# A graph network kernel: count rows gathered as 16-bit integers and turned by transposing transfers, and the mean's transposes moved amid the products of the node's own rows

## The reference, cut to what matters

```python
h = jnp.maximum(_layernorm(x, axis=-1), 0.0)
x = x + _L0_gnn_ref(h, edge_index, ...)           # attention over neighbours
h = jnp.maximum(_layernorm(x, axis=-1), 0.0)
x = x + _L1_gnn_ref(h, ...)

def _L1_gnn_ref(x, gate_W, gate_b, Wl, bl, Wr, edge_index):
    gates = softmax(x @ gate_W + gate_b); top_v, top_i = top_k(gates, 2)
    def sage_conv(h, W_l, b_l, W_r):
        aggr = segment_sum(h[src], dst) * inv_deg   # mean over neighbours
        return aggr @ W_l + b_l + h @ W_r
    for e in range(4):
        h = x
        for l in range(2):
            h = relu(sage_conv(h, Wl[e, l], bl[e, l], Wr[e, l]))
        ...
    out = sum of the two picked experts' h, each times its gate
```

## Time and profile before

| | us |
|---|---|
| median of 3 runs | 862.31 (857.92 to 866.23) |
| the profiled execution | 863.82 |
| its span, first to last instruction | 862.1 |
| TensorE busy | 752.3 (87%) |
| VectorE busy | 444.7 (52%) |
| ScalarE busy | 254.6 (30%) |
| POOL busy | 176.2 (20%) |

### The profile page before, as it was taken

One profiled execution on the slowest core, in us unless ns is written; L12 is line 12 of the kernel. 1 busy time (PEld: TensorE's weight loads), 2 busy tenths in 40 slices (PEclk: granted clock), 3 DMA queues, 4 the chain that ended last, 5 costly groups with the idle time before them and its releaser, 6 DMA issues.

```text
span 862.1 us, 11919 instructions
## 1 busy us (share of the span) xinstructions
PE 752.3 (87%) x3620; PEld 611.0 (71%) x3621; DVE 444.7 (52%) x1088; ACT 254.6 (30%) x516; POOL 176.2 (20%) x160
## 2 busy tenths in 40 slices
PE   1019877499997999998999999989999999999994
PEld 0007655388886888876777777768888888888883
DVE  6999999678876415572263343433223332323230
ACT  0113444555555425141141221312211221212120
POOL 6602433300000001055000000023322332233201
PEclk9999899889997999999999999999999999999997
DMA  4200000011124014769989695369934993449910
GB/s 127 84 0 2 0 0 0 1 59 59 62 84 149 2 49 127 241 195 275 304 285 331 223 348 172 105 197 272 327 94 109 274 330 93 110 108 246 343 22 5
DMA packets 46809, 125.30 MB, mean 145 GB/s; under 512 B 7280, under 2 KB 7412, under 8 KB 46752
## 3 DMA queue, kind: packets, MB, share of 16 engines
q1 hardware_dynamic: 29072, 81.58, 29.0%
q0 software_dynamic: 9232, 26.17, 12.1%
q10 hardware_dynamic: 8448, 16.78, 5.6%
HBM read 72.19 MB, written 53.20 MB: 145 GB/s over the span
## 4 chain that ended last, share of the span: by engine, by line
PE 71%; DVE 18%; DMA 4%; issue 3%; DVEq 1%; ACT 1%; POOL 0%; POOLq 0%; SPq 0%; ACTq 0%
PE ps L1417 15%; PE ps L1419 15%; PE ps L1418 15%; PE ps L1714 6%; PE ps L1713 5%; DVE onehot_g L1025 5%; PE ps L1579 3%; DVE column L1013 3%; PE ps L1580 3%; PE ps L1641 3%; DMA raw<-in_L_gnn_Wr 2%; DVE onehot_p L966 2%; PE ps L1685 1%; PE ps L1724 1%; PE ps L1510 1%
## 5 line engine op out<-in xcount | busy, mean ns | idle before, releaser
L1714 PE MATMUL ps<-slots,CTs 125*128 x230 | 90.9, 395 | 0.0
L1713 PE MATMUL ps<-slots,CTs 125*128 x207 | 81.6, 394 | 0.0
L1345 DVE CAST CTs<-ps 125x512 fp32r<-125x512 f32 (+1 forms) x69 | 37.3, 595 | 85.1 <-PE ps L1641 62.0
L611 POOL DMA_INDIRECT out<-tg,rec x23 | 36.9, 1605 | 192.3 <-ACT tg L877 175.5
L1252 DVE TENSOR_TENSOR he_t<-ps,b_b 125x512 f32<-125x512 f32 x40 | 27.5, 690 | 86.1 <-PE ps L1419 73.8
L1390 DVE TENSOR_TENSOR tm<-ps,b_b 128x512 f32<-128x512 f32 x23 | 15.9, 691 | 102.3 <-PE ps L1419 102.3
L1417 PE MATMUL ps<-W,h2T_hi 128*125 128x512 f32 x160 | 64.2, 401 | 2.8 <-DVE W L1220 2.8
L827 ACT ACTIVATE slots<-he_t 125x512 fp32r<-125x512 f32 x40 | 25.3, 635 | 132.3 <-DVE he_t L1252 113.3
L1418 PE MATMUL ps<-W,h2T_hi 128*125 128x512 f32 x160 | 63.8, 399 | 0.0
L1419 PE MATMUL ps<-W,h2T_lo 128*125 128x512 f32 x160 | 63.7, 398 | 0.0
L1417 PE MATMUL ps<-W,agT_hi 128*125 128x512 f32 x160 | 63.6, 397 | 0.0
(11 more groups left out here) (268 smaller groups left out, 1722.9 us busy)
## 6 DMA issues: line engine op xcount, KB each, us to landing
he_d<-slots SPq DMA_DIRECT2D x30, 448.0 KB
slots<-he_d SPq DMA_DIRECT2D x30, 448.0 KB
w_d<-slots SPq DMA_DIRECT2D x3, 4096.0 KB
slots<-w_d SPq DMA_DIRECT2D x24, 512.0 KB
t_d<-he_t SPq DMA_DIRECT2D x40, 224.0 KB
c_d<-c_nat SPq DMA_DIRECT2D x10, 546.9 KB
raw<-in_L_gnn_Wl ACTq DMA_DIRECT2D x4, 1024.0 KB
raw<-in_L_gnn_Wr ACTq DMA_DIRECT2D x4, 1024.0 KB
```

Source lines behind the costliest of these rows:

```text
L611: g.indirect_dma_start(out, bass.IndirectOffsetOnAxis(ap=i32(rec[:, i, 2:3]), axis=0), tg[i % 3][:], None, bounds_check=N - 1, oob_is_err= ...
L1345: v.tensor_copy(CTs[:, 4 * r:4 * r + n, :], ps[0:P, r, 0:n * S].rearrange("p (c n) -> p c n", n=S)).then_inc(cts_ready.sem, 1)
L1713: mm(o, CTs[:, t, :], part(k, P, t * 1024, P), start=False, stop=False)
L1714: last = mm(o, CTs[:, t, :], part(k, P, t * 1024 + D, P), start=False, stop=t == T - 1)
```

## The change

- `c_nat`, `c_d` and the gathered `crow` hold 16-bit integers. A row is 1280 numbers (ten blocks of 128, the last three of each are padding) in place of 1250: 2560 bytes in place of 5000. VectorE clears the padding once.
- `turn_rows(i)` leaves TensorE. ScalarE issues a transposing DMA, `crow` to a new buffer `CTi` (two of them), and VectorE's `counts_in` copies from `CTi` in SBUF in place of PSUM. `turn_rows(0)` is issued in the last expert of the first convolution, `turn_rows(1)` before the tile loop, `turn_rows(i+2)` at the end of ScalarE's part of tile i.
- The first gathers of counts wait for the second weight of the last expert being cut (`w_lo_ready`), no longer for `wl_done`. `b2_b` moves to where `crow` was, so SP's load of it waits for `wl_done`.
- `turn_means(i)` moves behind the first 6 of the 12 own-row products in `transformed(i)`.

```diff
-        crow = [at(f"crow_{k}", [S, N], F32, o) for k, o in enumerate((147456, 152480, row_at))]
+        crow = [at(f"crow_{k}", [S, T * S], I16, o) for k, o in enumerate((R4, R4 + 2560, row_at + 1536))]
+        CTi = [at(f"CTi_{k}", [S, T, S], I16, o) for k, o in enumerate((R4 + 5120, row_at - 1024))]
-        b2_b = at("b2_b", [S, NE, D], F32, R4)
+        b2_b = at("b2_b", [S, NE, D], F32, 147456)
-        c_d = nc.dram_tensor("c_d", [N, N], F32).ap()
+        c_d = nc.dram_tensor("c_d", [N, T * S], I16).ap()
 # SP
+            sp.wait_ge(*c_pad_ready(1))
             with sp.Fori(0, QN) as q:
...
                 else:
+                    sp.wait_ge(*wl_done(NE * NGR))
                     for p, e in enumerate(PO):
                         sp.dma_start(b2_b[:, p, :], ...)
 # POOL
-            pool.wait_ge(*wl_done(NE * NGR))
+            pool.wait_ge(*w_lo_ready(KC * (cut_number(NE - 1, 1) + 1)))
             for i in range(2):
                 gather_counts(i)
...
-                    pool.wait_ge(*crow_turned(3 * (i + 1)))
+                    pool.wait_ge(*cti_in[i % 2](16 * (i // 2 + 1)))
                     gather_counts(i + 3)
 # ScalarE
+            def turn_rows(i):
+                act.wait_ge(*crow_in[i % 3](16 * (i // 3 + 1)))
+                if i >= 2:
+                    act.wait_ge(*cts_ready(3 * (i - 1)))
+                act.dma_start_transpose(CTi[i % 2][:], crow[i % 3][:]).then_inc(cti_in[i % 2].sem, 16)
...
                     load_raw(x + 1, 1)
+                else:
+                    turn_rows(0)
                 hidden(x, 2)
             act.wait_ge(*l1_done(NE * T))
+            turn_rows(1)
...
                 mean_high(i)
+                if i + 2 < NT:
+                    turn_rows(i + 2)
 # VectorE
+            v.memset(c_nat[:].rearrange("p i (t n) -> p i t n", n=S)[:, :, :, P:], 0).then_inc(c_pad_ready.sem, 1)
...
+                dve.wait_ge(*cti_in[i % 2](16 * (i // 2 + 1)))
                 for r, n in enumerate(TURNS):
-                    dve.wait_ge(*crow_turned(3 * i + r + 1))
-                    v.tensor_copy(CTs[:, 4 * r:4 * r + n, :], ps[0:P, r, 0:n * S].rearrange("p (c n) -> p c n", n=S)
-                                  ).then_inc(cts_ready.sem, 1)
+                    v.tensor_copy(CTs[:, 4 * r:4 * r + n, :], CTi[i % 2][0:P, 4 * r:4 * r + n, :]).then_inc(cts_ready.sem, 1)
 # TensorE
-                        if x == NE - 1 and t == T - 1:
-                            pe.wait_ge(*pre_ready(x * T, GROUPS[NGR - 2][-1] + 1))
-                            turn_rows(0)
...
                     for c in range(KC):
+                        if j == 0 and c == KC // 2:
+                            turn_means(i)
...
                 neighbours(i, k, he_here)
-                if i + 1 < NT:
-                    turn_rows(i + 1)
                 if i == 0:
                     turn_hidden(i)
-                turn_means(i)
                 transformed(i, k, w2_here)
```

More of the change, by code:

```diff
@@ L19 @@
 I32 = mybir.dt.int32
+I16 = mybir.dt.int16
 ALU = mybir.AluOpType
@@ L208, in gnn_kernel @@
         ag1 = at("ag1", [P, 4, D], F32, R4 + 8192)
-        c_nat = at("c_nat", [P, 2, N], F32, R3 + 20480)
+        c_nat = at("c_nat", [P, 2, T * S], I16, R3 + 20480)
         slots = at("slots", [128, 2, 18432], F32R, 0)
@@ L256, in gnn_kernel @@
         assert o6[0] <= 40960
-        crow = [at(f"crow_{k}", [S, N], F32, o) for k, o in enumerate((147456, 152480, row_at))]
+        crow = [at(f"crow_{k}", [S, T * S], I16, o) for k, o in enumerate((R4, R4 + 2560, row_at + 1536))]
+        CTi = [at(f"CTi_{k}", [S, T, S], I16, o) for k, o in enumerate((R4 + 5120, row_at - 1024))]
+        assert R4 + 3 * 2560 <= R4 + 8192 and row_at + 1536 + 2560 <= fields_at
         CTs = at("CTs", [P, T, S], F32R, 157504)
@@ L304, in gnn_kernel @@
         crow_in = signals("crow_in0 crow_in1 crow_in2")
+        cti_in = signals("cti_in0 cti_in1")
         hrow_in = signals("hrow_in0 hrow_in1 hrow_in2 hrow_in3")
-        (crow_turned, cts_ready, ctl_ready, hrow_used, heT_hi_ready, heT_lo_ready, agg_done, agn_ready, agg_turned,
+        (c_pad_ready, cts_ready, ctl_ready, hrow_used, heT_hi_ready, heT_lo_ready, agg_done, agn_ready, agg_turned,
          aggT_hi_ready, aggT_lo_ready, tm_ready, tg_ready, settled) = signals(
-            "crow_turned cts_ready ctl_ready hrow_used heT_hi_ready heT_lo_ready agg_done agn_ready agg_turned "
+            "c_pad_ready cts_ready ctl_ready hrow_used heT_hi_ready heT_lo_ready agg_done agn_ready agg_turned "
             "aggT_hi_ready aggT_lo_ready tm_ready tg_ready settled")
@@ L729, in counts_out @@
                     act.wait_ge(*c_out(0, q * 64))
-                a.activation(c_nat[:, r // 3, r % 3 * 4 * P:(r % 3 * 4 + n) * P], ps[0:P, 6 + r % 2, 0:n * P],
-                             ACT.Copy, accum_out=deg_part[:, q * 6 + r:q * 6 + r + 1]).then_inc(c_nat_ready.sem, 1)
+                first = r % 3 * 4
+                c_rows = c_nat[:, r // 3, first * S:(first + n) * S].rearrange("p (t n) -> p t n", n=S)
+                a.activation(c_rows[:, :, 0:P], ps[0:P, 6 + r % 2, 0:n * P].rearrange("p (t n) -> p t n", n=P), ACT.Copy, accum_out=deg_part[:, q * 6 + r:q * 6 + r + 1]).then_inc(c_nat_ready.sem, 1)
             for g in range(NP * QN + 3):
@@ L827, in hidden @@
                     a.activation(HE[:, t, 0:D], he_t[:, (x * T + t) % 4, :], ACT.Relu).then_inc(he_hi_ready.sem, 1)
+            def turn_rows(i):
+                act.wait_ge(*crow_in[i % 3](16 * (i // 3 + 1)))
+                if i >= 2:
+                    act.wait_ge(*cts_ready(3 * (i - 1)))
+                    with act.If(beyond):
+                        act.wait_ge(*ctl_ready(3 * (i - 1)))
+                act.dma_start_transpose(CTi[i % 2][:], crow[i % 3][:]).then_inc(cti_in[i % 2].sem, 16)
+            beyond = counts_beyond(act)
             for i in range(4):
@@ L1342, in counts_in @@
                     dve.wait_ge(*agg_done(i))
+                else:
+                    dve.wait_ge(*wl_done(NE * NGR))
+                dve.wait_ge(*cti_in[i % 2](16 * (i // 2 + 1)))
                 for r, n in enumerate(TURNS):
-                    dve.wait_ge(*crow_turned(3 * i + r + 1))
-                    v.tensor_copy(CTs[:, 4 * r:4 * r + n, :], ps[0:P, r, 0:n * S].rearrange("p (c n) -> p c n", n=S)
-                                  ).then_inc(cts_ready.sem, 1)
+                    v.tensor_copy(CTs[:, 4 * r:4 * r + n, :], CTi[i % 2][0:P, 4 * r:4 * r + n, :]).then_inc(cts_ready.sem, 1)
                 with dve.If(beyond):
@@ L1351, in counts_in @@
                     for r, n in enumerate(TURNS):
-                        v.tensor_tensor(CTl[:, 4 * r:4 * r + n, :], ps[0:P, r, 0:n * S].rearrange(
-                            "p (c n) -> p c n", n=S), f32(CTs[:, 4 * r:4 * r + n, :]), ALU.subtract
-                                        ).then_inc(ctl_ready.sem, 1)
+                        v.tensor_tensor(CTl[:, 4 * r:4 * r + n, :], CTi[i % 2][0:P, 4 * r:4 * r + n, :],
+                                        f32(CTs[:, 4 * r:4 * r + n, :]), ALU.subtract).then_inc(ctl_ready.sem, 1)
             for x in range(NE):
@@ L1385, in biased @@
             def biased(i):
+                if i == 0:
+                    dve.wait_ge(*b2_in(16 * NE))
                 e = dve.value_load(tab_t[0:1, i:i + 1, 4:5], min_val=0, max_val=NE - 1)
@@ L1391, in biased @@
                                 ALU.add).then_inc(tm_ready.sem, 1)
-            dve.wait_ge(*b2_in(16 * NE))
             for s in t_out:
@@ L1629, in half @@
                 return last
[L1631 to L1643, removed]
             for x in range(NE):
```

1 line of the change is left out of this document (added).

## The result

| | before | after |
|---|---|---|
| median, us | 861.4 | 913.7 |
| span of the profiled execution, us | 862.1 | 912.6 |
| TensorE busy, us | 752.3 | 744.7 |
| largest term of the chain that is new | | DMA CTi, 10% |

The change made the kernel 5.97% slower: the ratio is 1.0597, 95% interval 1.0541 to 1.0654. The median before is of four executions here. The forecast was 844, range 836 to 864. TensorE has less work, as intended, and waits more.

A forecast was written before the change was run, and what follows sets the result against it. TensorE's steps were taken to bound the tiles. Terms -2.8 - 23.1 + 7.4 + 0.8 - 0.6 + 0.1 = -18.2 us took the median from 862.3 to 844, range 836 to 864.

The forecast's parts named there:

- The frame: Tiles 1 to 22: TensorE is busy 270.22 of 271.00 us, so a step taken off it pays until another chain is late.
- Set 0 and the gap before tile 9: Last expert of the first convolution: set 0's transposes leave TensorE, a gap losing 2.89 us goes; term -2.8 us.
- Tile 0: First tile of the loop: the mean's transposes now stand in the stream, 13th product 3.7 us after the first; +0.8 us.
- Sets 1 to 22 off TensorE, and the new wait: Count transposes: set 1 nothing, tiles 1 to 21 -23.1 us; new TensorE wait before the 13th product, 0.35 a tile, +7.4.
- The cover of the transposing transfer: From ScalarE's issue to VectorE's copies: transfer taken as 3 to 6 us; up to 10 us costs nothing.
- rival B: Transposing transfer starved while an expert is loaded: 20 us each, period 16.5 in 9 tiles, 889 us; chance 0.12.
- Rival A: Transposing transfer does its ten 128-column blocks one after the other: 13 us, period 13.0, 877 us; chance 0.08.
- VectorE's copies: Count copies from SBUF in each tile: as dear as from PSUM (1.62 us), 1 us spare; cheaper ones gain nothing.

## Why the prediction was wrong

**The frame** (TensorE's steps are the time in the tiles): right. 62 us of waits on the path moved the end by 50, after 11.8 of gain.

**Set 0 and the gap before tile 9** (-2.8): right for the gap, too large for what is left of it. In the changed kernel the last product of tile 8 starts at 558.22 and tile 9's first at 558.47. The own rows of tile 0 are turned at 569.62, 3.7 earlier than the earlier trace rows; but 1.9 of this is there already at the last product of tile 8, so 1.8 of the 2.9 us of the gap are left. The 1.9 belong to no term: that stage moves by more from execution to execution of kernels that are alike in it (the last products with the neighbours' sum start at 554.5, 548.4 and 550.9 in the kernel before and in its two variants).

**Tile 0** (+0.8): too small. TensorE had waited 3.55 and 1.60 us, and its products then came 0.43 us apart and not 0.23, up to 577.2. The 13th product came 5.8 us after the first, not 3.7. The prediction took distances from a tile at full clock, and the granted clock was at half, 1.2 GHz, from 573 to 577.2 (window below).

**Sets 1 to 22 off TensorE, and the new wait:** right in kind. A quiet tile of the changed kernel, TensorE:

```profile
636.18 0.60 PE L1731 MATMUL ps<-ident,agn 128*128 128x128 f32 x4
...
637.79 0.40 PE L1443 MATMUL ps<-slots,heT 128*128 x1
638.28 0.49 PE L1441 MATMUL ps<-slots,aggT 128*128 x1
...
640.95 0.40 PE L1443 MATMUL ps<-slots,aggT 128*128 x1
641.36 0.63 PE L1692 MATMUL ps<-ident,hrow 128*128 128x128 f32 x4
```

The first product with aggT starts 2.10 after the mean's transposes (2.21 forecast), after a wait of 0.26 and a restart that costs 0.1. The period is 11.77 and not 11.5: around the next tile's start 0.25 us are lost (here 0.41 from 640.95 to 641.36, where the kernel before has 0.24). The run with the move alone excludes the wait as its cause, and the last two periods, in which nothing more is gathered, are 11.52, the forecast's own. With the issue 6 us earlier and the own rows turned between the halves it seems gone too (11.3). What meets at that moment stays open.

**The cover of the transposing transfer:** this is the step that failed. "I take 3 to 6 us", with a cover of 10, is true of the quiet stretches (3.6 to 5.6) and false in a load (16 to 36), and so the new wait on `CTi`, which the sum has at nothing, was 62 us on the path. I compared its 328 KB with gathers in one stretch, that is, by bytes, and left the load to rival B. The page of the changed kernel counts pieces on ScalarE's queue:

```profile
q10 hardware_dynamic: 38624, 24.32, 11.3%
```

Before, that queue had 8448 pieces. The 30176 more are 1312 for each of 23 transfers, 82 on each of 16 engines, as rival B had reckoned but for the completions (80). The gathers have 128 long rows each. If each of the 82 waited in turn, it was 0.26 us for each (25 less 4, over 82), near the 0.22 that B had for one piece of 4096 bytes. The Trainium skill (DMA: Bandwidth & Descriptors, section "Queues, rings and completion order") says that a DMA engine takes turns between its queues packet by packet, and that a packet there is typically 9 to 17 descriptors. The runs at 4096 and 2048 bytes fit turns by the piece, those at 1024 and 512 do not go on in proportion, and no run shows how the pieces are put together into packets.

That the transfer waits piece by piece is argued, not shown, and one row speaks against it as the whole: POOL's gather of the same 328 KB in the first load took 20.6 us, with some 7 pieces on each engine (7760 on POOL's queue for 69 indirect transfers). One for one it would have been 2 us late, and it was 16 us late. What is shown is that the transfer is late when it meets a load, and less so when the load's pieces are shorter.

**Rival B** had the place and the wait, and I gave it 0.12. It forecast 889, nine tiles of 16.5; it was four tiles of 22 to 30. Two things made it dearer. In the first load the next transfer stood behind the late one: ScalarE's sequencer was in its issue for 13.1 us, until 601.2, and it landed 22.8 us after the first. And the granted clock was lower after each long wait that I looked at, down to half, 1.2 GHz (products 0.43 us apart, not 0.23). TensorE in the first long tile, where 12 products took 5.3 us (602.62 to 607.90) and not 2.9:

```profile
602.62 0.79 PE L1441 MATMUL ps<-slots,aggT 128*128 x1 [13.42 <-DVE aggT L1405]
603.21 0.63 PE L1442 MATMUL ps<-slots,aggT 128*128 x1
603.63 0.63 PE L1443 MATMUL ps<-slots,aggT 128*128 x1
...
607.90 0.64 PE L1692 MATMUL ps<-ident,hrow 128*128 128x128 f32 x4
```

The windows of the changed kernel say the same: in tile 0, in the first long tile, in the first load as a whole, and after it:

```profile
core 0: us, PE busy (x) PEld busy (x) DVE busy (x) ACT busy (x) POOL busy (x), PEclk, DMA share, GB/s
573.00:577.20 4.20, 4.20 (x14) 3.31 (x13) 0.69 (x1) 0.60 (x1) 0.36 (x1) 0.50 0.74 199
602.60:607.90 5.30, 5.28 (x13) 4.02 (x13) 0.00 (x0) 0.00 (x0) 0.00 (x0) 0.50 1.12 201
579.00:640.00 61.00, 38.47 (x158) 29.86 (x158) 9.16 (x18) 7.49 (x12) 10.90 (x9) 0.83 1.01 202
640.00:695.00 55.00, 54.42 (x244) 41.61 (x243) 14.75 (x29) 11.89 (x19) 17.50 (x15) 1.00 0.54 117
```

The evidence for B was in the prediction: full engines in three stretches. Against it I held that gathers make nobody wait there. They had three tiles of lead, so the rows could not show their latency; the transposing transfer had 10 us. A wait that isn't seen is no measure of a latency.

**Rival A** is refuted: ten blocks land in 4.4 us outside the loads. The Trainium skill (VectorE: DVE Perf Modes, section "The three transpose paths") gives 1309 ns for one block; by these landings ten blocks do not take ten times that, since 4.4 us leave at most 0.44 for each.

**VectorE's copies** from 16-bit numbers in SBUF took 0.96 us for three against 1.62, and gained nothing, as said.

**Small slips.** The bounds of the forecast's own range are reckoned over 22 tiles (7.7 and 6.6) where the sum has 21 (7.4 and 6.3), A's 0.8 is 0.74, and the chances of A and B add to 0.20, not 0.19. None of them matters beside the 62 us.

## What to carry to other kernels

Before work is moved from a busy engine to a transfer, reckon the transfer in pieces as well as in bytes, and take its time in the stretch where the engines are fullest. Here a transfer of many 256-byte pieces that lands in about 4 us outside the loads took 16 to 36 beside a bulk load of 4096-byte pieces, and four late tiles cost five times what the shorter period would have gained over all of them. A longer lead helps only when the transfer's own source comes as early, and an issue placed in a compute engine's list makes that engine wait for the source.

## What was not expected of the hardware

- In a load of 4096-byte pieces the indirect transfers were slow too, though they have few pieces: in the first load 20.6 and 21.0 us for gathers that land in 4.4 to 4.6 in a quiet stretch, in the other two 10 to 11.
- Shortening the load's pieces from 4096 to 2048 (with twice the issues) halved the wait for the first transposing transfer in a load (25 to 28 us, then 11 to 13); at 1024, with the issues as they were, it was 11 to 15 us.
- In the changed kernel ScalarE's sequencer was in the issue of a transposing transfer for 1.3 to 2.3 us in quiet stretches and up to 13.4 in a load.
- What stays open is the 0.25 us per quiet tile, why a gather of few pieces is as late in a load as it is, and what binds at pieces of 1024 bytes and less.
